# An attention row's products in another order on TensorE, and the query halves of every second pair of heads swapped

## The reference

```python
h = tok(x)                                  # patches -> 1024 hidden, silu -> 256
h = h + attn(_layernorm(h))                 # 16 heads of 16, softmax over the row's 128 tokens
h = h + ffn(_layernorm(h), ...)             # the two layers below

def _layer(x, wqkv, qs, ksc, wo, lg, lb, w1, b1, w2, b2):
    q, k, v = split(shift_token(x) @ wqkv)  # 8 heads of 64
    q, k = l2norm(q) * qs, l2norm(k) * ksc
    q, k = rotary_xpos(q, k)
    x = x + local_attention(q, k, v) @ wo   # window 128, causal
    h = layernorm(shift_token(x)) * lg + lb
    a, g = split(h @ w1 + b1)               # 2 x 682
    return x + (a * gelu(g)) @ w2 + b2
```

## Time and profile before

| | |
|---|---|
| median of 3 runs | 2650.95 us (2649.64 to 2651.02) |
| the profiled execution: its own time, its span | 2650.9 us, 2649.1 us |
| granted TensorE clock, mean | 0.994 |
| busy: TensorE, VectorE, ScalarE, GpSimd | 98%, 72%, 64%, 54% |

### The profile page before, as it was taken

How to read it: one execution, slowest core, us unless ns; L and a number is a source line. 1 busy time by engine, 2 the same in 40 slices (tenths; PEclk the granted TensorE clock), 3 DMA queues, 4 the chain that set the end, 5 groups by cost and what they waited for, 6 DMA issues and landing times.

```text
span 2649.1 us, 71437 instructions
## 1 busy us (share of the span) xinstructions
PE 2582.9 (98%) x25088; PEld 2221.2 (84%) x25088; DVE 1916.7 (72%) x3779; ACT 1702.0 (64%) x4184; POOL 1422.8 (54%) x1512
## 2 busy tenths in 40 slices
PE   7999999979999999999999999999999999999998
PEld 5888888868888888887888887888888887888887
DVE  7777777668778887786655556788877878666664
ACT  4666666658777777774444446787877777444442
POOL 7888888567777776662100006777777665000000
PEclk9999999989999999999999999999999999999999
DMA  2111111111111111112111111111111111222221
GB/s 47 39 47 37 45 37 37 42 44 39 52 39 50 39 38 42 56 39 79 50 60 56 53 34 49 38 52 39 50 41 36 42 59 34 80 80 73 77 72 48
DMA packets 167250, 130.39 MB, mean 49 GB/s; under 512 B 24870, under 2 KB 165320, under 8 KB 167093
## 3 DMA queue, kind: packets, MB, share of 16 engines
q1 hardware_dynamic: 164789, 119.81, 14.8%
q0 software_dynamic: 2304, 8.47, 1.1%
HBM read 77.47 MB, written 50.33 MB: 48 GB/s over the span
## 4 chain that ended last, share of the span: by engine, by line
PE 89%; DVE 4%; issue 3%; ACT 2%; POOL 1%; DMA 1%; SPq 0%; POOLq 0%; DVEq 0%; ACTq 0%
PE const_banks L1409 6%; PE const_banks L1411 6%; PE const_banks L1410 6%; PE const_banks L1401 6%; PE const_banks L1402 6%; PE const_banks L1403 6%; PE const_banks L1525 5%; PE const_banks L1463 5%; PE const_banks L1499 4%; PE const_banks L1555 3%; PE const_banks L1428 3%; PE const_banks L1429 3%; PE const_banks L1430 3%; PE const_banks L510 3%; PE const_banks L525 3%
## 5 line engine op out<-in xcount | busy, mean ns | idle before, releaser
L1107 ACT ACTIVATE attn_E<-const_banks,attn_nbias,attn_rn 128x128 f32<-128x128 f32 x1024 | 452.9, 462 | 137.8 <-DVE attn_nbias L1314 137.8
L1014 POOL TENSOR_TENSOR attn_qk<-attn_rot_a,attn_rot_b 128x1024 f32<-128x1024 f32 x128 | 303.3, 2370 | 343.3 <-issue 292.5
L1001 POOL TENSOR_TENSOR ffn_rstd<-ffn_var,const_neg_half 128x4 f32<-128x4 f32 x32 | 32.7, 1022 | 645.6 <-DVE ffn_var L1204 645.6
L1409 PE MATMUL const_banks<-weights_w_hi,attn_xT_hi 128*128 128x512 f32 x768 | 315.0, 410 | 3.8 <-ACT attn_sq L1142 3.3
L1411 PE MATMUL const_banks<-weights_w_hi,attn_xT_lo 128*128 128x512 f32 x768 | 303.4, 395 | 0.0
L1410 PE MATMUL const_banks<-weights_w_lo,attn_xT_hi 128*128 128x512 f32 x768 | 303.2, 395 | 0.0
L1225 DVE SCALAR_TENSOR_TENSOR ffn_gated<-const_banks,weights_b_col,ffn_gate 128x512 f32<-128x512 f32 (+1 forms) x192 | 143.7, 748 | 212.1 <-ACT ffn_gate L1085 204.2
L1401 PE MATMUL const_banks<-ffn_xT_hi,ffn_w_hi 128*128 128x512 f32 x704 | 281.7, 400 | 0.7 <-DVE ffn_gated L1225 0.7
L1402 PE MATMUL const_banks<-ffn_xT_lo,ffn_w_hi 128*128 128x512 f32 x704 | 277.9, 395 | 0.0
L1403 PE MATMUL const_banks<-ffn_xT_hi,ffn_w_lo 128*128 128x512 f32 x704 | 277.8, 395 | 0.0
L1085 ACT ACTIVATE ffn_gate<-const_banks,weights_b_col 128x512 f32<-128x512 f32 x160 | 110.0, 688 | 216.2 <-PE const_banks L1403 215.9
(11 more groups left out here) (181 smaller groups left out, 8003.6 us busy)
## 6 DMA issues: line engine op xcount, KB each, us to landing
attn_x_res<-xa SPq DMA_DIRECT2D x128, 128.0 KB, 4.9
xb<-attn_x_new SPq DMA_DIRECT2D x128, 128.0 KB, 1.7
ffn_x_<-xb SPq DMA_DIRECT2D x128, 128.0 KB
h<-ident_h SPq DMA_DIRECT2D x64, 128.0 KB, 1.7
xa<-ident_n SPq DMA_DIRECT2D x64, 128.0 KB, 1.7
attn_x_<-xa SPq DMA_DIRECT2D x128, 64.0 KB
xa<-ffn_x_new SPq DMA_DIRECT2D x16, 512.0 KB, 3.3
ffn_add<-h SPq DMA_DIRECT2D x16, 512.0 KB, 5.0
```

Source lines behind the costliest of these rows:

```text
L1014: pool.tensor_tensor(qk[:, slot].rearrange("p a n -> p (a n)"), rot_a[:].rearrange("p a h d -> p (a h d)"), rot_b[:].rearrange("p a h d -> ...
L1107: last = act.activation(E[:, r, i], ps_s[:, r, i * P:(i + 1) * P], ACT.Exp, bias=nbias[:, r, i:i + 1], scale=rn[:, slot, h:h + 1], accum_o ...
L1409: pe.matmul(out_, xT_hi[:, slot, k], w.w_hi[:, k, cols], start=(k == 0), stop=False)
```

## The change

The steady step on TensorE becomes: queries_keys, wo, values, transposes of qk, turn_row, weigh, transposes of E, masks and scores. The first four steps (`EARLY`) keep turn_row, x_high and x_low at their old places; later, x_high stands behind kT and x_low behind x_new, and x_new waits for xT_hi.

In the score tiles the pairs j = 1 and 3 hold the queries 64 to 127 in partitions 0 to 63 and the others in partitions 64 to 127. The masks follow, with the same number of columns. So that rn of a query still stands in its partition, ssm is written in four parts, the last two from one half of the partitions into the other. E's transposes come out with swapped columns, and weigh puts them back with two products of 64 columns where an odd pair's head had one of 128.

```diff
+        EARLY = (0, 1, 2, 3)
@@ ScalarE
-                if on(0) and not (layer and step in (0, 1)):
+                if on(0) and step in EARLY and not (layer and step in (0, 1)):
                     x_high(act, t, u)
...
                     act.activation(kT[:].rearrange("p k n -> p (k n)"), ps_k[:], ACT.Copy).then_inc(s["kT_done"], 1)
+                if on(0) and step not in EARLY:
+                    x_high(act, t, u)
@@ VectorE
-                if on(0) and not (layer and step in (0, 1)):
+                if on(0) and step in EARLY and not (layer and step in (0, 1)):
                     x_low(dve, t, u)
...
+                    need(dve, s["xT_hi"], min_int(t + 1, L + ROWS))
                     dve.tensor_tensor(x_new[:, slot], ps_x[:, D:2 * D], x_res[:, slot], ALU.add).then_inc(s["x_done"], 1)
+                if on(0) and step not in EARLY:
+                    x_low(dve, t, u)
                 if on(1):
...
                     dve.tensor_reduce(ss[:], sq[:], AX_X, ALU.add).then_inc(s["normed"], 1)
                     need(dve, s["normed"], 2 * b + 1)
-                    dve.tensor_tensor(ssm[:], ss[:], tiny[:], ALU.max).then_inc(s["normed"], 1)
+                    dve.tensor_tensor(ssm[:, HEADS:], ss[:, HEADS:], tiny[:, HEADS:], ALU.max)
+                    pairs, pairs_m, floor = [ap[:, 0:HEADS].rearrange("p (a b r) -> p a b r", b=2, r=2)
+                                             for ap in (ss, ssm, tiny)]
+                    dve.tensor_tensor(pairs_m[:, :, 0], pairs[:, :, 0], floor[:, :, 0], ALU.max)
+                    for to, of in ((slice(0, HD), slice(HD, P)), (slice(HD, P), slice(0, HD))):
+                        last = dve.tensor_tensor(pairs_m[to, :, 1], pairs[of, :, 1], floor[of, :, 1], ALU.max)
+                    last.then_inc(s["normed"], 1)
@@ TensorE, weigh
-                        last = pe.matmul(ps_v[r * HD:(r + 1) * HD, j * P:(j + 1) * P],
-                                         v[:, u, h * HD:(h + 1) * HD], ET[:, r, j], start=True, stop=True)
+                        own, head = slice(r * HD, (r + 1) * HD), v[:, u, h * HD:(h + 1) * HD]
+                        if j % 2 == 0:
+                            pe.matmul(ps_v[own, j * P:(j + 1) * P], head, ET[:, r, j], start=True, stop=True)
+                            continue
+                        pe.matmul(ps_v[own, j * P:j * P + HD], head, ET[:, r, j, HD:P], start=True, stop=True)
+                        last = pe.matmul(ps_v[own, j * P + HD:(j + 1) * P], head, ET[:, r, j, 0:HD], start=True,
+                                         stop=True)
@@ TensorE, body: the order
-                if on(0) and not (layer and step in (0, 1)):
+                if on(0) and step in EARLY and not (layer and step in (0, 1)):
                     need(pe, s["xT_lo"], t)
-                    need(pe, s["x_done"], t - 5)
                     turn_row(pe, t, i, u)
...
-                    queries_keys(pe, b, slot)
-
-                    values(pe, b, slot)
+                    queries_keys(pe, t - 1, (u - 1) % 2)
+                if on(5):
+                    b = t - 5
+                    need(pe, s["oT_hi"], b + 1)
+                    need(pe, s["oT_lo"], b + 1)
+                    need(pe, s["xT_lo"], min_int(t, L + ROWS))
+                    need(pe, s["x_done"], b)
...
+                    last.then_inc(s["out_ps"], 1)
+                if on(1) and not (layer and step == 1):
+                    values(pe, t - 1, (u - 1) % 2)
...
+                if on(0) and step not in EARLY:
+                    need(pe, s["xT_lo"], t)
+                    need(pe, s["x_done"], t - 5)
+                    turn_row(pe, t, i, u)
+                if on(4):
                     weigh(t, u)
+                if on(2):
+                    need(pe, s["exp_done"], 2 * (t - 2))
...
                 if on(3):
...
-                if on(4) and step != ROWS + 2:
-                    weigh(t, u)
@@ TensorE, masks and scores
-                            pe.matmul(ps_s[0:HD, r].rearrange("p (i n) -> p i n", n=P)[:, :, 0:HD], eye,
-                                      rule[:, :, 0:HD], start=True, stop=False, skip_group_check=True)
-                        pe.matmul(ps_s[HD:P, r].rearrange("p (i n) -> p i n", n=P)[:, :, HD:P], eye, rule[:, :, 0:HD],
-                                  start=True, stop=False, skip_group_check=True)
+                        quarters = ps_s[:, r].rearrange("p (a q n) -> p a q n", q=4, n=HD)
+                        edge = rule[:, :, 0:HD].rearrange("p (a b) n -> p a b n", b=2)
+                        pe.matmul(quarters[0:HD, :, 0:4:3], eye, edge, start=True, stop=False, skip_group_check=True)
+                        pe.matmul(quarters[HD:P, :, 1:3], eye, edge, start=True, stop=False, skip_group_check=True)
...
-                            pe.matmul(ps_s[0:HD, r, j * P:j * P + HD], qT[part, j, 0:HD], kT[part, j, 0:HD],
+                            few, all_ = (slice(0, HD), slice(HD, P)) if j % 2 == 0 else (slice(HD, P), slice(0, HD))
+                            pe.matmul(ps_s[few, r, j * P:j * P + HD], qT[part, j, 0:HD], kT[part, j, 0:HD],
                                       start=False, stop=True, skip_group_check=True)
-                            last = pe.matmul(ps_s[HD:P, r, j * P:(j + 1) * P], qT[part, j, HD:P], kT[part, j],
+                            last = pe.matmul(ps_s[all_, r, j * P:(j + 1) * P], qT[part, j, HD:P], kT[part, j],
                                              start=False, stop=True, skip_group_check=True)
```

More of the change, by code:

```diff
@@ L1478, in body @@
                 elif on(1):
-                    b, slot = t - 1, (u - 1) % 2
                     if step == 1:
                         pe.wait_ge(w.a_low, w.parts)
-                    queries_keys(pe, b, slot)
-                    values(pe, b, slot)
+                    queries_keys(pe, t - 1, (u - 1) % 2)
[5 more added lines that the diff above has]
+                    need(pe, s["x_done"], b)
+                    out_ = ps_x[:, D:2 * D]
+                    for k in range(KI):
+                        pe.matmul(out_, oT_hi[:, k], w.wo_hi[:, k], start=(k == 0), stop=False)
+                        pe.matmul(out_, oT_hi[:, k], w.wo_lo[:, k], start=False, stop=False)
+                        last = pe.matmul(out_, oT_lo[:, k], w.wo_hi[:, k], start=False, stop=(k == KI - 1))
+                    last.then_inc(s["out_ps"], 1)
+                if on(1) and not (layer and step == 1):
+                    values(pe, t - 1, (u - 1) % 2)
                 if step == ROWS + 1:
@@ L1501, in body @@
                         last.then_inc(s[turned], 1)
[L1502 to L1511, removed]
-                        pe.matmul(out_, oT_hi[:, k], w.wo_lo[:, k], start=False, stop=False)
-                        last = pe.matmul(out_, oT_lo[:, k], w.wo_hi[:, k], start=False, stop=(k == KI - 1))
-                    last.then_inc(s["out_ps"], 1)
-                if step == ROWS + 2:
-                    weigh(t, u)
+                if on(0) and step not in EARLY:
[3 more added lines that the diff above has]
+                if on(4):
+                    weigh(t, u)
+                if on(2):
+                    need(pe, s["exp_done"], 2 * (t - 2))
+                    if isinstance(t, int):
+                        pe.wait_ge(s["qT_done"], t - 1)
+                        pe.wait_ge(s["kT_done"], t - 1)
                 if on(3):
@@ L1527, in body @@
                 if on(2):
-                    need(pe, s["exp_done"], 2 * (t - 2))
-                    if isinstance(t, int):
-                        pe.wait_ge(s["qT_done"], t - 1)
-                        pe.wait_ge(s["kT_done"], t - 1)
-                if on(4) and step != ROWS + 2:
-                    weigh(t, u)
-                if on(2):
                     b = t - 2
```

6 lines of the change are left out of this document (3 added, 3 removed).

## The result

The changed kernel takes 2725.44 us (median of 4 runs, 2723.95 to 2726.14), the kernel before 2650.74 us in the same comparison (4 runs, 2649.64 to 2651.02). The ratio is 1.0282, with a 95% interval of 1.0267 to 1.0298: 2.8% slower. Forecast were 2716 us and a range of 2665 to 2738. The profiled execution took 2725.24 us, of which 2723.5 are the span, 74.4 us more than before's 2649.1.

A forecast was written before the change was run, and what follows sets the result against it. The prediction took a ScalarE-VectorE ring, not TensorE, as the bound at 10.03 us a step. Maxima 60.3 us, unrolled steps 4.8, filling and draining 0: together +65, from 2650.9 to 2716 us, range 2665 to 2738.

The forecast's parts named there:

- The ring: ScalarE and VectorE, exponentials through rot_b, squares, ss, ssm, neg_top, nbias to the next exponentials: sets the 10.03 us step.
- The maxima: VectorE between ss and neg_top: four maxima for one add 0.58 us a round, 60.3 us over 104 loop steps.
- The holds: VectorE: three handovers that change partition half start only after the predecessor ends, 0.20 us each.
- The unrolled steps: Some six steady steps per layer outside VectorE's loop: 0.4 us each, 4.8 us, TensorE's pace absorbing part of 0.58.
- Filling and draining: 0: First and last rows of a layer: no cost, the shorter scores set against wo's earlier place.
- TensorE's own step: TensorE's need per loop step: from 9.81 to about 9.72 us, scores 0.22 less, one border 0.13 more.
- The wait ahead of wo: TensorE in the loop: waits near 0.9 us for oT_lo before its first product with wo.
- x_high and x_low: Moved halves of x on ScalarE and VectorE: in time, cost 0, ScalarE free 0.2 us before the squares.
- No hold: Rival: the four maxima follow at 0.05 to 0.09 us, +18 us, 2669 us; chance 0.12.
- TensorE as the bound: Rival: the step follows TensorE and falls from 10.03 to about 9.75 us, -29 us, 2622 us; chance 0.07.
- it cancels: Rival: slack ahead of neg_top, its wait for the scores, takes the maxima in, 2651 us; chance 0.04.
- more than the maxima: Rival: the squares wait for ScalarE instead of rot_b, 0.3 us a round on top, +31, 2747 us; chance 0.08.

The follow-up runs named there:

- e4: Kernel before with only the changed kernel's four maxima, so scores are scaled with the other half's norms: 2714.81 us, ratio 1.0244.
- e1: Changed kernel with a single 128x16 maximum instead of four, so odd pairs' scores are scaled with the other half's norms: 2657.44 us, ratio 1.0027.
- e11: Changed kernel with the queries' three maxima moved behind oT_lo and rot_b ahead of the second scaling of E: 2648.07 us, ratio 0.9997.
- e12: Changed kernel's order with the score tiles, weigh and single maximum of the kernel before, and rot_b ahead of E's second scaling: 2657.41 us, ratio 1.0033.
- e2: Changed kernel with four maxima, the two odd-pair ones on all 128 partitions, no change of half, nothing swapped: 2682.73 us, ratio 1.012.
- e3: Changed kernel with the two odd-pair maxima each reading and writing its own half, leaving two changes of half: 2711.42 us, ratio 1.023.
- e5: Changed kernel with the four maxima moved behind nbias on VectorE: 2683.81 us, ratio 1.0133.
- e9: Kernel before with rot_b moved ahead of the second scaling of E on VectorE: 2704.94 us, ratio 1.021.
- e10: Changed kernel with only the keys' maximum ahead of neg_top and the queries' three behind oT_lo: 2666.37 us, ratio 1.0066.

## Why the prediction was right

**The ring as the bound, right.** e4 changes only VectorE's maxima and gives the step of 10.571; e1 changes them back and gives 10.045. TensorE's busy share, 96% in e4 and 97% in e1, told neither.

**The maxima, right in mechanism, a little too large.** The step of the sum was +0.58 us a round; measured are +0.53 from ss to neg_top and +0.54 a step. The holds came out as forecast, three of them, but a held handover of a 0.15 us maximum costs about 0.18 rather than 0.20. 104 steps came to 56 us instead of 60.3.

**The unrolled steps, right in size, wrong in reason.** 4.8 us had been put down for twelve steps; they cost some 6. TensorE's own pace was to absorb part of the 0.58 there. It absorbs nothing: rows 57 to 60 cost 0.54 each as in the loop, from 9.82 us to 10.36. The ring itself is 0.2 us shorter in unrolled steps, in e4 too (10.36), so the 9.81 that was read as TensorE's pace was as much the ring's.

**"Filling and draining: 0", wrong, and the largest miss.** It measures 2.0 + 1.1 + 9.4 = 12.5 us, and is what made 65 into 74 (56 in the loop, some 6 in the unrolled rows, 12.5 here). The term took wo's earlier place as a gain everywhere. In the draining, where 9.4 of the 12.5 lie, it is the reverse: wo stands at the head of a step that has no products before it, so its wait for oT_lo, 0.53 us under cover in the loop, is 3.94 us bare. Those rows, e1's same wait of 3.5 us and e4, which with the old order loses 0.2 us there, place the cost; no run moved wo back by itself, and the lower clock behind the wait is not priced apart. Of the 2.0 us ahead of the first nbias, e4 has 1.6 with the maxima alone; how they cost that much there stays open.

**TensorE's own step, wrong in sign, without consequence.** From 9.81 it was to go to 9.72 us; e11, in which TensorE waits for nothing, has 9.93. The scores shrank by the forecast 0.22 in this step (1007.60 to 1008.36 is 0.76 us, 1014.55 to 1015.53 in the trace before 0.98), and by 0.18 in the mean (0.79 against 0.97). What was mis-sized: weigh, taken at no cost for its split, takes from 1005.33 to the next work at 1006.44, 1.11 us, against 1013.39 to 1014.42, 1.03, in the trace before: +0.08; and a product with wo followed the transposes of q and k by 0.79 us (1180.32 to 1181.11 in the trace before), where weigh now follows at a border. By e12 the order alone costs about 0.2 us a step, and the swap gives 0.1 of that back. Sorting did not shorten TensorE's step.

**The wait ahead of wo, right in place, 0.53 us instead of 0.9,** for the most part for the same reason: TensorE itself needs 0.2 us more. **x_high and x_low, right:** the squares wait for rot_b and lose nothing, with 0.18 us to spare where 0.2 had been worked out.

**The rivals.** No hold (2669) is excluded by e2 against e3 (and cost more than it had put down: e2, with four maxima and no hold, takes 2683); TensorE as the bound (2622) by e4; it cancels (2651) by the step itself; more than the maxima (2747) by the squares' wait for rot_b. What the forecast missed altogether is what e5 to e9 showed: the ring is not alone. GpSimd's keys close a second one, which had about 1 us to spare, qT and the scores a third, and where VectorE's work meets GpSimd's decides how much a reordering really gives. The changed kernel ran into none of these. The forecast had given them one clause on GpSimd's keys and no sum, so that part was luck.

## What to carry to other kernels

Find the ring before you cut work: start at an instruction that recurs, step from releaser to releaser, and compare the round with the free-running step of the busiest engine. When an edit adds small instructions, price them by where they stand and by whether they change partitions, not by their size: four maxima of 256 to 1024 elements cost 2.4% here. Before moving work out of one ring, follow who else consumes its result, and price a reordering in the draining steps too, where nothing covers its waits.

## What the hardware showed that was not expected

- **A tiny VectorE instruction held by GpSimd.** nbias went from 0.17 to 0.78 us in e9 and a 128x4 maximum from 0.15 to 0.85 us in e10, each ending within 0.03 us of a GpSimd tensor instruction that was running when it started. The Trainium skill, "SBUF — State Buffer", SBUF: two separate sides, describes the port pair that VectorE and GpSimd share as an exclusive lock, whose loser is blocked fully rather than slowed; these rows agree with it. Not every GpSimd instruction holds them up: in the kernel before all 40 nbias of the stretch start while GpSimd computes rn (1016.04 + 1.64, nbias at 1017.28) and last 0.17 us. A lock held for the whole of such an instruction does not show there, and the rows decide.
- **The other way round.** GpSimd's add of rot_a and rot_b takes 2.37 us in the mean of its 128 in the kernel before, 2.38 in the changed one, and 2.87 in e9, e11 and e12, the three with rot_b first (2.90 in e9's row above). In e11 it starts at 997.43, beside VectorE's scaling of E at 997.41; that the two hold each other up is argued from these rows, not tried.
- **A change of half has a price of its own.** Unheld, a small maximum costs 0.08 us; held, 0.18. The ladder of steps is 10.045 (one maximum), 10.245 (four, no change), 10.47 (two changes), 10.575 (three).
